# Edge network with segment maxima on one core: nodes regrouped in 224s, maxima gathered group by group, four short pairs at the end

## What is computed

```python
h = jnp.maximum(_layernorm(x, axis=-1), 0.0)
e_feat = jnp.concatenate([h[src], h[dst], edge_attr_32], axis=-1)     # 400000 x 96
v = jax.nn.relu(e_feat @ W1 + b1) @ W2 + b2                           # 96 -> 64 -> 32
x_cand = jax.ops.segment_max(v, dst, num_segments=12500)
out = x + jnp.maximum(x_cand, h)
```

## Time and profile before

| | |
|---|---|
| median of three runs | 4759.54 us (4758.01 to 4763.21) |
| span of the profiled execution, first to last instruction | 3219.5 us |
| median less that span | 1540.0 us |
| busy: PE, PEld, DVE, ACT, POOL | 93%, 69%, 68%, 66%, 75% of the span |
| granted TensorE clock, mean | 0.970 of full speed |

### The profile page before, as it was taken

How to read it: one execution, slowest core, us unless ns; L and a number is a source line. 1 busy time by engine, 2 the same in 40 slices (tenths; PEclk the granted TensorE clock), 3 DMA queues, 4 the chain that set the end, 5 groups by cost and what they waited for, 6 DMA issues and landing times. The chain is left out here.

```text
span 3219.5 us, 56263 instructions
## 1 busy us (share of the span) xinstructions
PE 3007.4 (93%) x19600; PEld 2221.8 (69%) x19600; DVE 2189.0 (68%) x2420; ACT 2124.3 (66%) x2489; POOL 2408.5 (75%) x2547
## 2 busy tenths in 40 slices
PE   7999999999999999999999999999998998999910
PEld 5776677777777777777777777777776775777700
DVE  6321677777777777777777777777775775777743
ACT  4335677777777777777777777777775775777710
POOL 6777777777777777777777777777777777777756
PEclk9999999999999999999999999999999998999965
DMA  8940333333333333333333333333333333333321
GB/s 270 359 172 27 85 101 101 101 100 98 96 97 98 100 99 100 100 102 100 88 99 98 100 97 101 100 98 80 112 98 85 100 82 95 95 97 98 86 51 26
DMA packets 194362, 337.82 MB, mean 105 GB/s; under 512 B 74114, under 2 KB 118100, under 8 KB 193711
## 3 DMA queue, kind: packets, MB, share of 16 engines
q1 hardware_dynamic: 112264, 291.52, 26.6%
q0 software_dynamic: 81216, 41.73, 10.2%
q10 hardware_dynamic: 738, 3.21, 0.3%
HBM read 227.85 MB, written 108.41 MB: 104 GB/s over the span
## 5 line engine op out<-in xcount | busy, mean ns | idle before, releaser
L558 POOL DMA_INDIRECT src_in<-h_dram,src_ix x2293 | 2167.0, 945 | 698.8 <-issue 637.8
L794 PE MATMUL ps_rows<-onehot,table 128*128 128x512 f32 x9800 | 2290.4, 393 | 28.0 <-DVE onehot L1054 28.0
L794 PEld LDWEIGHTS ps_rows<-onehot,table 128*128 128x128 f32 x9800 | 1832.3, 189 | 501.8 <-issue 107.2
L719 ACT ACTIVATE onehot<-distance 128x1024 fp32r<-128x1024 bf16 x882 | 878.8, 1049 | 696.8 <-PE ps_rows L794 696.8
L714 ACT ACTIVATE distance<-picks,below_column 128x1024 bf16<-128x1024 int16 x882 | 954.8, 1136 | 49.3 <-DMA picks<-picks_dram 49.3
L1054 DVE SCALAR_TENSOR_TENSOR onehot<-picks,column,ps_layers 128x1024 fp32r<-128x1024 int16 x392 | 493.0, 1278 | 356.2 <-PE ps_rows L794 340.6
L1104 DVE STREAM_TRANSPOSE ps_layers<-rows_in 128x512 f32<-128x512 f32 x196 | 129.5, 706 | 236.6 <-ACT hid L705 198.3
L1108 DVE TENSOR_TENSOR_SCAN dst_t<-mask_in,dst_t,ps_layers 128x512 f32<-128x512 bf16 x196 | 251.0, 1280 | 7.0
L705 ACT ACTIVATE hid<-ps_layers,b_col 128x512 f32<-128x512 f32 x392 | 234.0, 674 | 28.1 <-PE ps_layers L824 28.1
L1121 DVE TENSOR_TENSOR_SCAN max_t<-mask_in,max_t,ps_layers 128x512 f32<-128x512 bf16 x192 | 245.4, 1278 | 3.5
L1125 DVE STREAM_TRANSPOSE rows_in<-max_t 128x512 f32<-128x512 f32 x196 | 210.8, 1115 | 3.4
(11 more groups left out here) (112 smaller groups left out, 1102.3 us busy)
## 6 DMA issues: line engine op xcount, KB each, us to landing
picks<-picks_dram SPq DMA_DIRECT2D x98, 512.0 KB
first_rows<-hid SPq DMA_DIRECT2D x100, 500.0 KB, 4.1
rows_in<-in_edge_attr_dram SPq DMA_DIRECT2D x97, 512.0 KB
rows_in<-first_rows SPq DMA_DIRECT2D x97, 512.0 KB
run_max<-rows_in SPq DMA_DIRECT2D x96, 512.0 KB
src_in<-h_dram,src_ix POOLq DMA_INDIRECT x2293
mask_in<-mask_dram SPq DMA_DIRECT2D x97, 256.0 KB
h_dram<-h_sb ACTq DMA_DIRECT2D x1, 1568.0 KB
```

The costliest lines, as they stand in the source:

```text
L558: pool.indirect_dma_start(out=src_in[:, slot, g, r, :], out_offset=None, in_=rows[:, :], in_offset=bass.IndirectOffsetOnAxis(ap=src_ix[:, ...
L719: nc.scalar.activation(onehot[:, RING_AT[c] + BY_DVE[c] + k, :, :].rearrange("p g w -> p (g w)"), distance[:, k, :], ACT.Relu, bias=1.0, s ...
L794: mm = nc.tensor.matmul(ps_rows[g][side][:, 0:WIDE], table[:, i * SIDES + side, part, :], onehot[:, RING_AT[c] + t, g, :], start=(i + part ...
```

## The change

1. **Short pairs.** There are now 101 pairs: 96 of 1,024 edges a lane, pair 96 (`SHORT_AT`) of 672, and four (`MINIS`) of 256. The 256 edges of a short pair are all looked up; none is gathered. `layer_one_mini` and `layer_two_mini` work on 256 columns. PE does 101 look-ups instead of 98, POOL 24 source gathers fewer.
2. **Nodes in groups.** A column group `hb` now holds 224 consecutive nodes (`GROUP`) of each quarter of 3,136 nodes (`QUAD`), seven to a partition. x, h and out are read and written in pieces of seven rows (896 bytes). The start that follows a partition's seventh node lies in the next partition, so `starts_packed` is sent round to `wrapped` by 11 small transfers, and the 14 last columns of the groups are scattered after all others (`place_edges`).
3. **Maxima by group.** The gathers of maxima follow POOL's last source gathers, into slots of `src_in`. Groups 0 to 10, 11 and 12 wait for a number of stored pairs which `find_levels` and `find_need` work out; group 13 waits for all.
4. **Clearing.** The last 20,000 rows of each lane of `run_max` are set to zero before (`maxima_cleared`): four transfers of 2.56 MB.
5. **Lane borders.** `carried` and its six operations for two groups go. After all output is stored, POOL gathers the three border nodes from `out`, DVE takes a maximum, and POOL scatters them back. Output is stored by group, four transfers each, 55 in all, the three of the last group with 32 full partitions and two more for its rest.

```diff
+MINIS = 4
+MINI = 2 * PICKED
+SHORT_AT = (LANE - MINIS * MINI - SHORT) // (2 * BLK)
+PAIRS = SHORT_AT + 1 + MINIS
+LEVELS = [(0, NHB - 3), (NHB - 3, NHB - 2), (NHB - 2, NHB - 1)]
+LOW_TURNS = 5
+LOW_ROWS = LOW_TURNS * P * ZCOL // F
@@ SP, set-up
             clear(60, ZDMAS)
             load_indices(AHEAD, 1, ix_loaded[1])
+            for a in range(A):
+                unset = run_max[STARTS[a] + LANE - LOW_ROWS:STARTS[a] + LANE, :].rearrange("n f -> (n f)")
+                sp.dma_start(unset.rearrange("(p z c) -> p z c", p=P, c=ZCOL),
+                             zeros[:, :].unsqueeze(1).broadcast_to([P, LOW_TURNS, ZCOL])).then_inc(maxima_cleared, D)
             all_cleared(sp)
             sp.wait_ge(start_rows_read, D)
...
+            sp.wait_ge(packed_made, NHB + 1)
+            for a in range(A):
+                q = (a + 1) * LANES - 1
+                sp.dma_start(wrapped[a * LANES:q, :], starts_packed[a * LANES + 1:q + 1, :]).then_inc(starts_wrapped, D)
...
+            sp.wait_ge(maxima_cleared, A * D)
             sp.wait_ge(rows_scattered, D * NJ)
@@ SP, end
+            for hb in range(NHB):
                 sp.wait_ge(out_made, hb + 1)
+                group = slice(hb, hb + 1)
+                for a in range(A - (hb == NHB - 1)):
+                    sp.dma_start(by_group(out, a, group), grouped(out_sb, a, group)).then_inc(out_written, D)
...
+            sp.wait_ge(fixed_written, D)
@@ POOL, end
-            all_stored(pool)
+            for n, (lo, hi) in enumerate(LEVELS):
+                pairs_needed = pool.value_load(need_i[0:1, n:n + 1], min_val=1, max_val=PAIRS)
+                pool.wait_ge(pairs_stored, pairs_needed)
+                for hb in range(lo, hi):
+                    gather_maxima(hb)
+            pool.wait_ge(pairs_stored, PAIRS)
+            for hb in range(LEVELS[-1][1], NHB):
+                gather_maxima(hb)
+            pool.wait_ge(out_written, D * OUT_STORES)
+            pool.indirect_dma_start(out=bound_out[:, :], ... in_=out[:, :] ...).then_inc(bound_out_read, D)
+            pool.wait_ge(fixed_made, 1)
+            pool.indirect_dma_start(out=out[:, :], ... in_=fixed[:, :], in_offset=None).then_inc(fixed_written, D)
@@ PE, end
-            for slot in range(2):
-                layer_one(PAIRS - 2 + slot, slot, False, slot == 1)
-                layer_two(PAIRS - 2 + slot, ps_rows[slot], True)
+            for j in range(SHORT_AT, PAIRS - 2):
+                pair(j, j % 2, short=j == SHORT_AT, mini=j > SHORT_AT)
+            for j in range(PAIRS - 2, PAIRS):
+                layer_one_mini(j, j % 2, False, j == PAIRS - 1)
+                layer_two_mini(j, ps_rows[j % 2], True)
```

More of the change, by code:

```diff
@@ L528, in _ @@
+            for k in range(2 * AHEAD):
+                feed(k, k, 0, settled=k >= 2)
+            with sp.Fori(1, DOUBLE_TURNS - 2) as i:
                 for k in range(2 * AHEAD):
                     feed(i * (2 * AHEAD) + k, k, i)
-            for turn in range(DOUBLE_TURNS - 2, DOUBLE_TURNS):
-                for k in range(2 * AHEAD):
-                    j = turn * 2 * AHEAD + k
-                    feed(j, k, turn, loads=j + 2 < PAIRS, picks=j + 3 < PAIRS, indices=j + 2 * AHEAD - IX_AT < PAIRS, end=j == PAIRS - 2,
-                         before_last=j == PAIRS - 3, last=j == PAIRS - 1, last_indices=j + 3 * AHEAD - IX_AT == PAIRS)
@@ L672, in _ @@
                 stage_edge(b)
[L673 removed]
+            act.wait_ge(node_ready, A + 1)
             for j in range(NJ):
@@ L815, in layer_one @@
                 pe.wait_ge(src_turned, j * 2 + 2)
-                gathered = [GATHERED, LAST_GATHERED if last else GATHERED]
+                gathered = [GATHERED, SHORT_GATHERED if short else GATHERED]
                 for g in range(2):
@@ L1155, in _ @@
                 one_hot(0, 0, c)
-            place_last()
+            place_edges()
             find_side(0, 0)
@@ L1162, in _ @@
             find_side(1, 1)
+            place_last()
+            find_levels()
+            compare_bounds()
             dve.wait_ge(raw_step, 8 * RAW_PAIRS)
```

570 lines of the change are left out of this document (362 added, 208 removed).

## The result

| | before | after | ratio |
|---|---|---|---|
| beside each other, four runs each | 4758.77 us (4756.87 to 4763.21) | 4805.38 us (4795.45 to 4811.14) | 1.0102 [1.0085, 1.0118] |
| profiled execution of after | | span 4803.0 us for a time of 4804.81 us | |

The change costs 46.6 us. The forecast was 4760 us within 4740 to 4772; the measured time lies 33 us above that range.

A forecast was written before the change was run, and what follows sets the result against it. POOL was taken as the bound. Gathers moved off the end (-113.7 us) were offset by look-ups (81.7 less 11.3), set-up (25.5) and stores and borders (some 18): +0.9, 4760 us, own range 4750 to 4769, with rivals 4740 to 4772.

The forecast's parts named there:

- I apply the difference to the median, since 1540.0 us lie outside the span in either case: Last step: the span's change of +0.9 us was added to the median time, giving 4760 us.
- the sum: Whole span: all gains and costs of the change together, 3220.4 us against 3219.5, +0.9 us.
- POOL as the bound: Whole kernel: POOL never idle for 3,057 us, needing 30.0 us a pair against PE's 27.7; its set-up delays reach PE's end.
- Clearing and the hold: Set-up: four clears of maxima ahead of the start rows leave POOL idle 25.5 us (22 to 28).
- The queue rule: Set-up, SP's queue: each DMA engine takes a ring's descriptors in order, so start rows wait for the clears before them.
- Rival A: Set-up: start rows do not wait for the clears; 7.3 us in place of 25.5, 4742 us; chance 0.20.
- Three look-ups: PE's last pairs: three added look-ups cost 27.7, 27.0 and 27.0 us, 81.7 in all.
- The last passes: After the look-ups: two layer passes on 256 columns take 9.5 us instead of 20.8 (bounds 8 and 12).
- 91 maxima behind other work: End: 91 of 98 gathers of maxima move into POOL's idle time beside PE's last look-ups, taking away 113.7 us.
- The end: Output: 55 stores 0.45 us apart, the last at 3208.2, then 12.2 us of border mending to the span's end.
- Rival B: End, SP's queue: stores 0.64 us apart, so the last starts 10.3 us later; 4771 us; chance 0.17.
- rival C: End: the levels hold all maxima until the last pair, about +97 us, 4857 us; chance 0.03.

The follow-up runs named there:

- b1: The kernel before, unchanged, run on a starved (slow) occasion: 4753.95 us, 1.0000 of before.
- a1: The changed kernel, unchanged, run on the same starved occasion as b1: 4806.66 us, 1.0105 of before.
- e_late: The changed kernel with all 98 gathers of maxima waiting for the last stored pair, starved occasion: 4816.57 us, 1.0121 of before.
- e_pace: The changed kernel with each two groups of maxima (14 gathers) waiting for a look-up's first tile, quick occasion: 3241.18 us, 1.0054 of before.
- e_order: The changed kernel with the clears of maxima issued after the start rows, quick occasion: 3214.71 us, 0.9973 of before.
- e_split: The changed kernel with the 101-partition store of picks cut into 96 and 5, quick occasion: 3228.41 us, 1.0016 of before.
- near copies: e_pace and the changed kernel with SLACK set from 6 to -1, quick occasion: 3241.18 and 3242.08 us against 3224.03 of before.
- b0: The kernel before, unchanged, run on a quick occasion: 3222.37 us, 0.9998 of before.

## Why the prediction was wrong, point by point

**The failed step** of the prediction is "I apply the difference to the median, since 1540.0 us lie outside the span in either case". They lay inside. In every starved execution the span is the time less 2 to 7 us (4803.0 for 4804.81 in after, 4746.4 for 4751.94 in b1). The 3219.5 us were another execution than those timed, and the account made in it was carried to executions in which other things are slow: there the 84 gathers put beside the last pairs cost PE 80.0 us (a1 against b1; 93.4 against e_late), a cost that the sum put at nothing. The gap of a third between a span and its median was the sign: no launch cost of that size had a row.

**POOL as the bound.** "Whatever delays POOL in the set-up by x delays PE's end by x" is right for the quick kind: e_pace's hold is 27.3 us longer than e_order's and its time 26.5 us, and e_split's is 12.8 shorter than e_pace's and its time 12.8. In the starved kind the tie is the other way round: POOL waits for PE, and PE's stalls beside POOL's bursts set the distances, 43 us a pair in the main loop and 51 in pairs 90 to 93.

**Clearing and the hold**, 25.5 us (22 to 28): 29.4 in after, 30.8 in a1. In the quick kind 39.8, of which 12.8 us are the store of 101 partitions; without them 27.0. The term was right for the four clears; the store's new partition count the forecast did not name at all. The queue rule of the Trainium skill, page "DMA: Bandwidth & Descriptors", section "Queues, rings and completion order", which the forecast leaned on, is borne out: with the start rows ahead of the clears of maxima the hold is 12.5 us (e_order), behind them 39.8. Rival A (the start rows don't wait) is refuted. In the starved kind pair 0 starts only 11.8 us later. The likely reason is that PE searches at full pace while POOL is held, and stands when POOL scatters. The windows of a1 show both, and one of e_pace (quick kind, the last row) shows PE at work beside the same scatters (us, busy and count of PE, PEld, DVE, ACT, POOL, granted clock, DMA share, GB/s):

```profile
240.00:250.00 10.00, 10.00 (x75) 7.13 (x74) 0.88 (x3) 3.47 (x10) 0.00 (x0) 1.00 1.02 397
250.00:260.00 10.00, 10.00 (x75) 7.12 (x74) 3.94 (x12) 3.07 (x12) 0.00 (x0) 1.00 1.02 396
...
310.00:320.00 10.00, 0.85 (x2) 0.10 (x1) 0.00 (x0) 0.00 (x0) 7.56 (x9) 0.50 0.06 13
320.00:330.00 10.00, 0.00 (x0) 0.00 (x0) 0.00 (x0) 0.00 (x0) 7.56 (x9) 0.50 0.05 13
```

```profile
310.00:320.00 10.00, 10.00 (x45) 8.28 (x45) 3.21 (x8) 6.97 (x8) 7.56 (x9) 1.00 0.10 25
```

**Three look-ups**, 81.7 us: 81.4 in a1 (27.73, 27.73, 28.1, 26.63 and 26.64 less two pairs of b1), 81.0 in e_split (27.70, 26.65, 26.63). **The last passes**, with what follows until the gathers, 11.3 us less: 8.1 less.

**91 maxima behind other work**, -113.7: they did leave the end, but a row was missing in the account. "Where POOL sat idle" was taken as free; it is free for POOL. PE pays 80.0 us for it in the starved kind. No other term of the account is off by as much.

**The end.** 55 stores at 0.45 us, measured 25.69 for 55, 0.467 each, a1; there are two more stores that the forecast did not count, so it is 26.1 us from the first to the last instead of 24.3. From the last store to the end of the span come 15.1 us instead of 12.2. The last gathers are held by SP and not by POOL, as said; the end is 40.8 us behind their start, forecast 36.3. Rival B (0.64 us) is refuted, rival C too: 84 of the 91 maxima were gathered by the start of pair 94.

**Were the sum at least right where it was made?** Not quite: +0.9 there against +17 for the near copies, 13 of them the store of 101 partitions. The changed kernel itself was never run in the quick kind. e_split, which lacks that store's cost, is the nearest to what the forecast describes: first scatter at 228.3 (226 to 230 forecast), last source gather at 3065.4 (3066.5), first of the last seven gathers at 3187.8 (3184.1), span 3228.4 (3220.4). Of the 8.0 us that are left 4.3 are the end, above. The path up to it is 3.7 late; pairs 94 and 95 alone add 4.9 (30.9 and 29.4 us instead of 27.73; in the first DVE waits 6.3 us for gathered rows).

## What to carry to other kernels

Before a sum is made from a profile, its span must be about the time that is to be forecast; where it is not, the profile is of something else, and the first question is which engine would make up the difference. An idle engine is free to use only if its work holds up no other: indirect transfers issued back to back were put into idle time of POOL, and in the starved kind PE stood still beside them. Where a size becomes a partition count of a transfer (here pairs, 98 to 101), look at what stands behind that transfer in its queue.

## What was not expected of the hardware

- **One program, two speeds, by the occasion.** 3223 and 4757 to 4855 us for the kernel before, mean granted clock 0.97 and 0.82 to 0.83, each steady to 0.7% within an occasion. What decides between them stays open, and so does the part of the recording, whose semaphore events are 21 to 23 thousand in the starved kind and 56 to 57 thousand in the quick one.
- **Beside back-to-back indirect transfers of POOL the other engines stand still** in the starved kind, at 13 GB/s of traffic (windows above): in 320 to 330 PE, DVE and ACT do nothing (PE waits for ACT there, and ACT stands still too). While a burst lasts, PE starts single products at distances of 0.70, 1.40, 2.10 and 2.80 us; in a1's pairs it recovers 2.4 to 4 us after the burst's end. In the quick kind such bursts cost nothing: beside 65 gathers of maxima e_order's pairs 96 to 98 take 27.70, 26.65 and 26.63 us, the same as in e_late, where none stand beside them. The trace names no releaser.
- **The granted clock follows the starvation.** In those windows it is 0.50 (1.2 GHz) after PE has stood idle, 1.00 (2.4 GHz) when PE was busy throughout. The average look-up takes 418 ns in after and 393 in e_order. How much of the 1,526 us between the spans of b0 and b1 is clock and how much is waiting was not taken apart.
- **A store of 101 partitions** (404 KB) holds up four clears behind it for 15 us; as 96 and 5 it does not. Its 101 packets start one at a time, 0.155 us apart.
